# Block sums of two graph convolutions held in PSUM, one-hots made by ScalarE, landings passed on by SyncE

## The reference

```python
def gcn_conv(x, W, b, src, dst, n_nodes):
    h = x @ W
    ...
    norm = dinv[src] * dinv[dst]
    msg = h[src] * norm[:, None]
    agg = jax.ops.segment_sum(msg, dst, num_segments=n_nodes)
    agg = agg + h * (dinv * dinv)[:, None]
    return agg + b
...
h1 = jax.nn.relu(gcn_conv(embedding, W1, b1, src, dst, n))
h2 = jax.nn.relu(gcn_conv(h1, W2, b2, src, dst, n))
...
k = _ln(k, kln_g, kln_b)
v = _ln(v, vln_g, vln_b)
kv = jnp.einsum('bhnd,bhne->bhde', k, v) / HW
...
h = jax.nn.gelu(ret @ w1 + b1, approximate=False)
return h @ w2 + b2 + bias
```

## Time and profile before

| | us |
|---|---|
| median of 3 runs | 5891.33 |
| lowest and highest | 5884.73 to 5892.93 |
| the profiled execution's span | 5935.3 |
| of it, convolution 0's gathers | 2878 to 4012 |
| convolution 1's gathers | 4089 to 5221 |

### The profile page before, as it was taken

One profiled execution on the slowest core, in us unless ns is written; L12 is line 12 of the kernel. 1 busy time (PEld: TensorE's weight loads), 2 busy tenths in 40 slices (PEclk: granted clock), 3 DMA queues, 4 the chain that ended last, 5 costly groups with the idle time before them and its releaser, 6 DMA issues. The chain is left out here.

```text
span 5935.3 us, 66919 instructions
## 1 busy us (share of the span) xinstructions
PE 3546.3 (60%) x13782; PEld 2710.2 (46%) x13783; DVE 2982.8 (50%) x6982; ACT 1018.9 (17%) x2146; POOL 3055.9 (51%) x2888
## 2 busy tenths in 40 slices
PE   4744455454389865998444544454445454466998
PEld 3633233232267654776433433333434444455666
DVE  5466566666899964445433333334333333354443
ACT  0111121121179801221000000000000000013121
POOL 1266677676368624221466666663666666612111
PEclk9877767776599976998566566655555555566999
DMA  4487666666578762223311111111111111123221
GB/s 108 136 217 211 202 207 203 204 206 195 158 227 271 224 188 88 63 63 97 106 28 28 29 28 28 29 29 32 28 29 28 28 29 28 29 62 98 70 87 37
DMA packets 432122, 617.01 MB, mean 104 GB/s; under 512 B 100329, under 2 KB 309161, under 8 KB 431721
## 3 DMA queue, kind: packets, MB, share of 16 engines
q1 hardware_dynamic: 304733, 389.03, 21.1%
q0 software_dynamic: 107440, 200.97, 14.1%
q10 hardware_dynamic: 19852, 25.94, 1.6%
HBM read 419.67 MB, written 209.64 MB: 106 GB/s over the span
## 5 line engine op out<-in xcount | busy, mean ns | idle before, releaser
L1857 POOL DMA_INDIRECT big<-t_d,src_tiles x1564 | 1483.7, 949 | 957.2 <-issue 450.8
L2080 PE MATMUL v_bank<-big,v_oh 128*128 x3328 | 716.2, 390 | 1216.6 <-issue 830.3
L2080 PEld LDWEIGHTS v_bank<-big,v_oh 128*128 128x128 f32 x3328 | 674.7, 300 | 1302.8 <-issue 1302.2
L653 POOL DMA_INDIRECT big<-xl_d,src_steps x832 | 859.8, 1033 | 378.1 <-issue 356.0
L1935 DVE TENSOR_TENSOR big<-big,v_bank 128x64 f32 x1664 | 366.5, 220 | 1285.3 <-DMA xj_d<-big 973.2
L759 PE MATMUL se_z_ps<-big,se_oht 128*128 x1664 | 608.7, 517 | 628.5 <-issue 385.9
L759 PEld LDWEIGHTS se_z_ps<-big,se_oht 128*128 128x128 f32 x1664 | 386.8, 250 | 850.4 <-issue 780.7
L692 DVE TENSOR_TENSOR se_z<-se_z_ps,big 128x528 f32<-128x528 f32 x416 | 291.4, 700 | 461.1 <-DMA es_ts<-src_p 256.8
L1122 PE MATMUL ae_bank<-ae_v,ae_oh 128*128 128x266 f32 x1664 | 402.3, 397 | 49.8 <-DVE big L1106 36.7
L1081 POOL TENSOR_TENSOR ae_v<-ae_v,ex 128x1792 f32<-128x1792 f32 x104 | 334.1, 3215 | 178.1 <-DMA ae_v<-xj_d 178.0
L1122 PEld LDWEIGHTS ae_bank<-ae_v,ae_oh 128*128 128x128 f32 x1664 | 310.4, 191 | 141.5 <-DVE big L1106 53.0
(11 more groups left out here) (468 smaller groups left out, 5316.9 us busy)
## 6 DMA issues: line engine op xcount, KB each, us to landing
xj_d<-big SPq DMA_DIRECT2D x208, 528.0 KB
ae_v<-xj_d SPq DMA_DIRECT2D x208, 528.0 KB
se_dlb<-dlr_d SPq DMA_DIRECT2D x104, 256.0 KB
big<-t_d,src_tiles POOLq DMA_INDIRECT x1564
buf_d<-ne_blank SPq DMA_DIRECT2D x4, 4112.0 KB
e_xs<-buf_d SPq DMA_DIRECT2D x106, 129.0 KB, 2.1
big<-xl_d,src_steps POOLq DMA_INDIRECT x832
cp_y<-y_d SPq DMA_DIRECT2D x14, 896.0 KB, 7.4
```

The lines of the kernel that those rows point to most:

```text
L653: nc.gpsimd.indirect_dma_start(half_of(u)[:, k, :], None, table, bass.IndirectOffsetOnAxis(ap=m.src[:, t:t + 1], axis=0)).then_inc(landed[ ...
L1857: nc.gpsimd.indirect_dma_start(rows[:, t % RING, :], None, table, bass.IndirectOffsetOnAxis(ap=m.srct[:, t:t + 1], axis=0)).then_inc(lande ...
L2080: last = nc.tensor.matmul(bank[u][:, k * MH:(k + 1) * MH], oh[:, u, k, :], of_block(rows, at[k]), start=True, stop=True)
```

## The change

The sums of all 49 blocks now stay in PSUM. Seven banks (`sums`, PB = 7) hold 49 x 64 numbers for each partition. `seed` puts the nodes' own rows there with matmuls by the identity, `total` adds each product in place (start=False, with a register for the block, loaded on TensorE), and `close` ends each bank's group of matmuls with a product of zeros. VectorE's `add` is gone. All else that TensorE makes goes into the eighth bank, `mixb`, and into the unused end of the seventh. In convolution 1 `up` and `down` share `mixb`, so `up(k)` waits in addition for `finish(k-1)` and stands behind the odd group's sums. The column sums of the keys are 128 x 1 products, and are spread at the end.

ScalarE makes the one-hots, eight times Abs and one Relu, in the same two buffers under the same wait. GpSimd has four landing semaphores, waits for landings only from g = 4, and no longer counts `tiles_in` up; SyncE does that (`pass_on`), behind its load of `xt`, which has two buffers now. `refresh` reads PSUM in seven pieces of eight blocks, and `hand_over` copies convolution 1's sums to `m.agg`. The loops of TensorE and SyncE are unrolled by two.

```diff
+PB = (NB * MH + 511) // 512
...
-        xt = sb("xt", [P, D])
-        bank = [ctx.enter_context(nc.psum_tensor(f"v{which}_bank{i}", [P, 512], F32)) for i in range(8)]
-        landed = [s["in0"], s["in1"]]
-        iota = bank[3 + which][:, 0:P]
+        xt = sb("xt", [P, 2, D])
+        zero = sb("zero", [1, 512], BF16)
+        sums = ctx.enter_context(nc.psum_tensor(f"v{which}_sums", [P, PB, 512], F32))
+        mixb = ctx.enter_context(nc.psum_tensor(f"v{which}_mixb", [P, 512], F32))
+        sum_of = sums[:, :, :].rearrange("p c (b n) -> p (c b) n", n=MH)
+        tail = sums[:, PB - 1, :]
+        flat_table = m.table.rearrange("p b n -> p (b n)")
+        in_bank = lambda c: slice(c * 512, min((c + 1) * 512, NB * MH))
+        blocks_in = lambda c: slice(c * (512 // MH), min((c + 1) * (512 // MH), NB))
+        s = {n: m.sem(f"v{which}_" + n) for n in "in0 in1 in2 in3 tiles_in oh_apart oh_ready summed zeroed closed xt0 xt1 weights".split()}
+        landed = [s[f"in{u}"] for u in range(4)]
         table = m.t_d.rearrange("b p n -> (b p) n")
+        xt_in = [s["xt0"], s["xt1"]]
...
-                    if g >= 2:
-                        pool.wait_ge(landed[g % 2], 16 * GS * (g // 2))
-                        pool.sem_inc(s["tiles_in"], 1)
+                    if g >= 4:
+                        pool.wait_ge(landed[g % 4], 16 * GS * (g // 4))
                     if g + NB // GS + 2 > RING // GS:
                         pool.wait_ge(s["summed"], g + NB // GS + 2 - RING // GS)
                     for t in range(g * GS, min((g + 1) * GS, NT)):
                         nc.gpsimd.indirect_dma_start(rows[:, t % RING, :], None, table,
-                                                     bass.IndirectOffsetOnAxis(ap=m.srct[:, t:t + 1], axis=0)).then_inc(landed[g % 2], 16)
-                for g in (TG - 2, TG - 1):
-                    pool.wait_ge(landed[g % 2], 16 * (GS * (g // 2) + min(GS, NT - g * GS)))
-                    pool.sem_inc(s["tiles_in"], 1)
+                                                     bass.IndirectOffsetOnAxis(ap=m.srct[:, t:t + 1], axis=0)).then_inc(landed[g % 4], 16)
+                for g in range(TG - 4, TG):
...
                 def load(k, u, r):
-                    if at_least(k, 1):
-                        sp.wait_ge(mixed, k)
-                    sp.dma_start(xt[:, :], block_rows(m.xnt_d, k)).then_inc(s["xt_in"], 16)
-                pipeline(sp, NB, 1, (0, load))
+                    if at_least(k, 2):
+                        sp.wait_ge(mixed, k - 1)
+                    sp.dma_start(xt[:, u, :], block_rows(m.xnt_d, k)).then_inc(xt_in[u], 16)
+                def pass_on(k, u, r):
+                    for i in range(2):
+                        short = 2 * k + i == TG - 1 if isinstance(k, int) else False
+                        sp.wait_ge(landed[2 * u + i], 16 * (GS * r + (NT - (TG - 1) * GS if short else GS)))
+                        sp.sem_inc(s["tiles_in"], 1)
+                pipeline(sp, NB, 2, (0, load), (1, pass_on))
...
+                V.memset(zero[:, :], 0.0).then_inc(s["zeroed"], 1)
...
-                def one_hot(g, u):
-                    if at_least(g, 2):
-                        dve.wait_ge(s["summed"], g - 1)
-                    V.tensor_tensor(oh[:, u, :, :], iota.unsqueeze(1).to_broadcast([P, GS, P]),
-                                    m.dl[:, bass.ds(g * GS, GS)].unsqueeze(2).to_broadcast([P, GS, P]),
-                                    ALU.is_equal).then_inc(s["oh_ready"], 1)
-
-                def add(g, u):
-                    dve.wait_ge(s["summed"], g + 1)
-                    blocks = blocks_of(nc, m, mybir.EngineType.DVE, g * GS, GS)
-                    for k in range(GS):
-                        t = g * GS + k
-                        if at_least(t, 1):
-                            dve.wait_ge(s["added"], t)
-                        V.tensor_tensor(of_block(m.agg, blocks[k]), of_block(m.agg, blocks[k]), bank[u][:, k * MH:(k + 1) * MH],
-                                        ALU.add).then_inc(s["added"], 1)
...
+                def spread_sums():
+                    dve.wait_ge(s["closed"], PB)
+                    V.tensor_copy(skw[:, :, :], tail[:, MH + KC * (P + 1):MH + KC * (P + 2)].unsqueeze(2).to_broadcast([P, KC, P]))\
+                        .then_inc(s["sk_wide"], 1)
...
+                        if c == PB - 1:
+                            dve.wait_ge(s["sums_out"], KC)
+                        if c < PB:
+                            V.tensor_tensor(part(m.agg, c), part(sum_of, c), dinv(c), ALU.mult).then_inc(s["scaled"], 1)
...
+                def hand_over():
+                    dve.wait_ge(s["closed"], PB)
+                    for c in range(0, PB, 2):
+                        V.tensor_copy(m.agg[:, blocks_in(c), :], sum_of[:, blocks_in(c), :])
...
-                    pipeline(dve, NR, 1, conv[0], conv[1], (1, variance, NB), conv[2], conv[3], (1, scale, NB), (0, add_bias, NB))
+                    pipeline(dve, NB, 1, (1, variance), (1, scale), (0, add_bias))
+                    spread_sums()
                     refresh()
                 else:
                     fold()
                     dve.wait_ge(s["weights"], 32)
-                    pipeline(dve, NR, 1, conv[0], conv[1], (1, normalise, NB), conv[2], conv[3], (1, finish, NB))
+                    pipeline(dve, NB, 1, (0, normalise), (0, finish))
+                    hand_over()
...
+                def one_hot(g, u):
+                    if at_least(g, 2):
+                        act.wait_ge(s["summed"], g - 1)
+                    for k in range(GS):
+                        nc.scalar.activation(oh[:, u, k, :], m.iota[:, :], ACT.Abs, bias=m.dl[:, bass.ds(g * GS + k, 1)],
+                                             scale=-1.0).then_inc(s["oh_apart"], 1)
+                    act.wait_ge(s["oh_apart"], GS * (g + 1))
+                    nc.scalar.activation(oh[:, u, :, :], oh[:, u, :, :], ACT.Relu, bias=m.ones[:, 0:1], scale=-1.0)\
+                        .then_inc(s["oh_ready"], 1)
...
+                    pipeline(act, NR, 1, even, (1, root, NB), odd, (0, square, NB))
+                    act.wait_ge(s["sk_wide"], 1)
...
+                    pipeline(act, NR, 1, even, odd, (0, gelu, NB))
+                    act.wait_ge(s["closed"], PB)
+                    for c in range(1, PB, 2):
+                        nc.scalar.copy(m.agg[:, blocks_in(c), :], sum_of[:, blocks_in(c), :]).then_inc(s["agg_out"], 1)
+                    act.wait_ge(s["agg_out"], PB // 2)
...
                 def total(g, u):
                     pe.wait_ge(s["oh_ready"], g + 1)
-                    if at_least(g, 2):
-                        pe.wait_ge(s["added"], GS * (g - 1))
                     tiles = tiles_needed(nc, m, mybir.EngineType.PE, g)
                     at = slots_of(nc, m, mybir.EngineType.PE, g * GS, GS)
+                    to = blocks_of(nc, m, mybir.EngineType.PE, g * GS, GS)
                     pe.wait_ge(s["tiles_in"], tiles)
                     for k in range(GS):
-                        last = nc.tensor.matmul(bank[u][:, k * MH:(k + 1) * MH], oh[:, u, k, :], of_block(rows, at[k]),
-                                                start=True, stop=True)
+                        last = nc.tensor.matmul(of_block(sum_of, to[k]), oh[:, u, k, :], of_block(rows, at[k]), start=False, stop=False)
                     last.then_inc(s["summed"], 1)
...
-                        nc.tensor.matmul(bank[4 + q][:, 0:P + 1], vn[0:rows_, q * P:(q + 1) * P], kn[0:rows_, q, :],
-                                         start=first, stop=final)
-                        last = nc.tensor.matmul(bank[6 + q][:, 0:P], m.ones[0:rows_, :], kn[0:rows_, q, 0:P],
-                                                start=first, stop=final)
+                        nc.tensor.matmul(vk_of(q), vn[0:rows_, q * P:(q + 1) * P], kn[0:rows_, q, :], start=False, stop=False)
+                        last = nc.tensor.matmul(sk_of(q), kn[0:rows_, q, 0:P], m.ones[0:rows_, 0:1], start=False, stop=False)
...
                 def up(k, u, r):
-                    pe.wait_ge(s["xt_in"], 16 * (k + 1))
+                    pe.wait_ge(xt_in[u], 16 * (r + 1))
                     if at_least(k, 1):
                         pe.wait_ge(s["ht_ready"], k)
+                        pe.wait_ge(s["mixed"], k)
                     for j in range(KC):
                         for q in range(KC):
-                            last = nc.tensor.matmul(bank[2][:, j * P:(j + 1) * P], m.m2[:, q, j * P:(j + 1) * P],
-                                                    xt[:, q * P:(q + 1) * P], start=(q == 0), stop=(q == KC - 1))
+                            last = nc.tensor.matmul(mixb[:, j * P:(j + 1) * P], m.m2[:, q, j * P:(j + 1) * P],
+                                                    xt[:, u, q * P:(q + 1) * P], start=(q == 0), stop=(q == KC - 1))
...
+                def nothing(c, start, stop):
```

(21 more changed lines are left out.)

75 lines of the change are left out of this document (35 added, 40 removed).

## The result

The changed kernel took 5948.52 us (median of 4 runs, 5936.64 to 5956.26), the kernel before 5891.09 in the same measurement: a ratio of 1.0099, 95% interval 1.0086 to 1.0113. It is slower by 57 us, where 5890 had been forecast. The profiled execution of the changed kernel, 5934.6 us long, is the fastest of its four. That of before was 5935.3, 44 us over its median, so the two spans as such say nothing.

A forecast was written before the change was run, and what follows sets the result against it. GpSimd's gathers were taken as the bound, their cadence kept (chance 0.43). Loop terms were nothing; -9.9 + 6 + 2.8 + 2 = +0.9 us on the median 5891.3 gave 5890, range 5690 to 6040.

The forecast's parts named there:

- What bounds the kernel: In both convolutions: GpSimd's gathers set the time, and its pauses, 311 us together, are what can be won.
- Rival B: Among the gathers: lateness belongs to the chain over VectorE, so the pauses go; -311 us, 5580; chance 0.22.
- TensorE's results are seen late while gathers are issued: Among the gathers: TensorE's results are seen late, and each GpSimd pause, near 3.5 us, lets two groups through.
- Adds and one-hots leave VectorE: In the loop: about 3.9 us a group leaves VectorE, lying under the gathers; likeliest gain none.
- One-hots on ScalarE: In the loop: one-hots cost ScalarE 3.6 to 4.25 us a group, hidden under the gathers.
- TensorE: In the sums: third table load and a register instruction per matmul cost nothing, at most +9.3 us a group.
- Rival C: Among the gathers: TensorE becomes the bound as its groups spread; +110 us, 6000; chance 0.27.
- Seeds: Before GpSimd's first wait, 69 us after its start: seven fp32 matmuls and one of zeros, 14 us, hidden.
- Landings: SyncE's passing on holds up no sum; GpSimd's freed wait is worth 7.6 us at most.
- D: Only the landings matter: GpSimd loses its 7.6 us of waits for gathers; 5884; chance 0.08.
- Tails: Behind each convolution's gathers: last groups gain 6.6 and 3.3 us; with closing, copies and spreading, +0.9 us.
- The anchor: Whole kernel: the profiled 5935.3 us ran 44 us above the median for all stages, so 5891.3 was the base.

The follow-up runs named there:

- gathers_alone: The changed kernel without TensorE's sums over edges, ScalarE's one-hots and GpSimd's wait for sums; 5903.17 us, gathers 1069.1 and 1067.9 us.
- dve_onehots: The changed kernel with its one-hots on VectorE again, between the parts of the mix; 5902.53 us, 1.0019 of the kernel before.
- scalar_only: The kernel before with only the one-hots moved to ScalarE, in the changed kernel's order, adds staying on VectorE; 5896.71 us, 1.0014.
- change_gpsimd_passes: The changed kernel with GpSimd instead of SyncE adding to tiles_in, two groups behind, four landing semaphores kept; 5906.53 us, 1.0038 of the kernel before.
- landings_only: The kernel before with only the change's landings, two xt buffers and TensorE's and SyncE's loops unrolled by two; 5926.58 us, 1.0065.

## Why the prediction was wrong

- **What bounds the kernel.** "What can be won there is GpSimd's pauses", 311 us, failed. The floor of 977.5 us was the issue rate of a short burst; gathers in a long row take 1068 us. Rival B, at 0.22 and -311 us, could not happen: with the sums and every wait for them left out the gathers took 103 us less. The steady "16 gathers, a pause" was read from one place too: the trace it comes from has 61 pauses in convolution 0, many of them 8 gathers apart, and 49 periods would be all groups, the first six included.
- **TensorE's results are seen late while gathers are issued.** Right, and shown by `gathers_alone`. Right too that GpSimd waits for `summed`: at 101 of 108 stops in the trace before, a gather starts 0.26 us after its update. That a pause is what lets the results through is not shown: in `gathers_alone` they come through, 29 us late, with hardly a pause. "Two groups a pause, as many as there are buffers" is at least incomplete: with two buffers `dve_onehots` issues 16 to 64 gathers in a row, mostly 24 to 48.
- **Adds and one-hots leave VectorE.** No gain in the loop was right: VectorE lost nearly three quarters of its work (from 743 to 209 us) for nothing there.
- **One-hots on ScalarE.** Their cost was right to the nanosecond (388 ns, 1.15 us), "hidden" wrong. I summed busy times and did not follow ScalarE's queue, where the next one-hots stand behind square or gelu of the same step. The order of instructions shown ahead of the prediction held it. This step failed: its term in the sum was 0, and the order measured about 25 us (1.0038 to 0.9994), with some 8 us more for the move itself (`scalar_only`). The Trainium skill ("ScalarE: Activation LUTs", Rules for kernel authors) would leave relu and the like to VectorE; `scalar_only`, at 1.0014, agrees in sign, though the queue costs more than the instructions.
- **TensorE.** Rightly set at nothing: `change_gpsimd_passes`, with all of the longer queue, has gathers of 1120.1 and 1120.5 us. Rival C named a time of 6000 and the right sign, but its mechanism is refuted: in convolution 1 slow groups fell from 34 to 3, and no period is held by TensorE. What spoke against C, "convolution 0 shows no singles", was misread: 17 of its 94 groups take over 5 us before, 24 after. That 5948.5 lies inside 5690 to 6040 is luck, since only C stretched the range that far.
- **Seeds.** Hidden, as forecast: with them, `change_gpsimd_passes` takes 1120.1 us for convolution 0's gathers. The sign that was to show it didn't come, since GpSimd's first wait stands 57 us after its start, a group earlier than the 69 us before.
- **Landings.** "Worth the 7.6 us at most", and D at 0.08. This is the step that failed most: the term was put at nothing, and it was the largest of all, +36 (1.0099 to 1.0038) to +38 us (`landings_only`). I looked at what GpSimd waits for, not at the form in which its two waits reach the DMA.
- **Tails.** Forecast +0.9 us, seeds and copies included. They measured +14.3 (4.4 and 9.9), since eleven groups at 5.0 us became pairs at 15 to 16 us, through ScalarE's order. With the order and the landings put right, they are 126.1 us against 134.6. The seven products of `close`, put at 3 us, took 3.2.
- **The anchor.** The profiled execution's excess of 44 us was subtracted as if it were spread over all stages. 26.7 us of it lay in the two convolutions, so "3.5 us pauses" in the changed profile looked like no change.

## What to carry to other kernels

Before a pause is counted as time to be won, take away what is waited for: here two thirds of the pauses came back, as longer gathers and longer gaps between them. Follow each moved instruction to its place in the new engine's queue, and ask what it now stands behind in the same step, however idle that engine is. And where an instruction waits twice, look in the built program or the trace for the wait that it carries itself; it should be the one that lasts. The order in the source doesn't tell: here `summed` was written last in the slow kernels too.
